# Batch 0's value projection moved ahead of the first scores, and each unit's value transfer put first on SyncE's queue

## The reference

```python
s = attention(xn)             # 32 heads of 8, keys i-8 .. i+7 alone, scores weighted by distance
                              # softmax, times the values, then proj_w and proj_b
g = silu(moe(xn))             # each token's best of 8 experts (router_w), silu-gated, score
                              # sigmoid(max logit), plus a shared expert for all tokens
out = x + s * g
```

## Time and profile before

| what | us |
|---|---|
| median of 3 runs | 641.51 (639.12, 641.51, 642.87) |
| the profiled execution, own time | 641.16 |
| its span | 639.3 |
| PE busy in the span | 562.8 (88%) |
| DVE busy | 404.0 (63%) |
| ACT busy | 308.1 (48%) |
| POOL busy | 186.8 (29%) |

### The profile page before, as it was taken

One profiled execution on the slowest core, in us unless ns is written; L12 is line 12 of the kernel. 1 busy time (PEld: TensorE's weight loads), 2 busy tenths in 40 slices (PEclk: granted clock), 3 DMA queues, 4 the chain that ended last, 5 costly groups with the idle time before them and its releaser, 6 DMA issues. The chain is left out here.

```text
span 639.3 us, 10599 instructions
## 1 busy us (share of the span) xinstructions
PE 562.8 (88%) x3358; PEld 484.0 (76%) x3358; DVE 404.0 (63%) x853; ACT 308.1 (48%) x762; POOL 186.8 (29%) x160
## 2 busy tenths in 40 slices
PE   2879999969879999999999999999886868789865
PEld 1657888858757899898999898898775756677754
DVE  6655746886755455455455455456688888886773
ACT  1374654557773544543544634546454543635332
POOL 6000101147861011010010110014645545532230
PEclk9899999979998999999999999999989899989997
DMA  9415532112326667666567576443133333330110
GB/s 294 133 62 190 177 122 61 57 44 96 111 87 178 174 166 223 196 184 195 165 189 223 167 218 185 134 133 107 51 98 110 102 106 105 113 109 20 43 35 23
DMA packets 107370, 82.89 MB, mean 130 GB/s; under 512 B 42292, under 2 KB 104756, under 8 KB 107316
## 3 DMA queue, kind: packets, MB, share of 16 engines
q1 hardware_dynamic: 98628, 68.72, 36.6%
q0 software_dynamic: 3072, 8.39, 4.1%
q10 hardware_dynamic: 5616, 5.11, 2.3%
HBM read 59.12 MB, written 23.07 MB: 129 GB/s over the span
## 5 line engine op out<-in xcount | busy, mean ns | idle before, releaser
L425 POOL TENSOR_TENSOR Sx<-Sx,mx 128x752 f32<-128x752 f32 x64 | 93.7, 1464 | 414.9 <-DVE mx L725 414.8
L941 PE MATMUL psV<-VB,PTs 128*128 128x132 f32 x1024 | 137.3, 288 | 43.3 <-DMA VB<-v_dram 19.0
L941 PEld LDWEIGHTS psV<-VB,PTs 128*128 128x128 f32 x1024 | 130.1, 197 | 50.8 <-issue 50.0
L468 ACT ACTIVATE Or<-psV 32x128 f32<-32x128 f32 x256 | 68.5, 268 | 151.4 <-DVE rs L755 148.9
L916 PE MATMUL psS<-kBD,qBD 128*128 128x188 f32 x512 | 104.9, 329 | 0.0
L916 PEld LDWEIGHTS psS<-kBD,qBD 128*128 128x128 f32 x512 | 87.9, 195 | 10.8 <-issue 2.0
L747 DVE STREAM_TRANSPOSE PTs<-Sx 128x512 f32<-128x512 f32 x128 | 82.9, 685 | 1.0 <-ACT Sx L498 1.0
L991 PE MATMUL psM<-xT,EB 128*128 128x128 f32 x624 | 76.4, 276 | 0.0
L718 DVE TENSOR_TENSOR Sx<-psS,cst 128x752 f32<-128x752 f32 x64 | 59.7, 933 | 26.3 <-PE psS L916 26.2
L991 PEld LDWEIGHTS psM<-xT,EB 128*128 128x128 f32 x624 | 73.9, 192 | 2.1 <-ACT qBD L487 1.3
L732 DVE SCALAR_TENSOR_TENSOR ea<-et,psM 128x256 f32<-128x256 f32 x39 | 16.4, 421 | 76.3 <-PE psM L991 47.2
(11 more groups left out here) (107 smaller groups left out, 690.6 us busy)
## 6 DMA issues: line engine op xcount, KB each, us to landing
EB<-in_L_ffn_gate_w SPq DMA_DIRECT2D x39, 256.0 KB, 3.0
EB<-in_L_ffn_up_w SPq DMA_DIRECT2D x39, 256.0 KB, 3.5
EB<-in_L_ffn_down_w SPq DMA_DIRECT2D x39, 256.0 KB, 3.1
VB<-v_dram SPq DMA_DIRECT2D x256, 32.0 KB
stage<-xs_dram SPq DMA_DIRECT2D x39, 128.0 KB, 2.2
ys_dram<-yb ACTq DMA_DIRECT2D x39, 128.0 KB, 3.1
xs_dram<-blank SPq DMA_DIRECT2D x9, 512.0 KB, 3.1
v_dram<-vS SPq DMA_DIRECT2D x8, 512.0 KB, 3.0
```

Source lines behind the costliest of these rows:

```text
L425: nc.gpsimd.tensor_tensor(s, s, mx[n % 3][:, :].unsqueeze(2).broadcast_to([P, 2 * G, KW]), ALU.subtract).then_inc(a_sub, 1)
L468: return nc.scalar.activation(dst, src, ACT.Copy)
L941: last = mm(psV[:, j, at:at + HS * VW], PTs[n % 2][:, k, j, i, :], VB[n % 2][:, i, k, :, VW * j:VW * j + VW], start=k == 0, stop=k == 1)
```

## The change

It does two things. First, the 4 value tiles of batch 0 are projected ahead of step 0, behind q, k0 and k1, by PE and by ACT, and stand in the list of jobs at that place; steps 1 to 7 keep theirs. Second, from SP's step 10 on (n - 1 > 8), `spread_v(n-1)` is the first thing of SP's step and no longer the last. For n - 1 = 0 to 8 it stays where it was, behind `keep_v`.

```diff
--- before.py
+++ after.py
@@ -113,7 +113,7 @@
 def jobs_of(n):
 
     if n == -1:
-        return [("tp", 0), ("tp", 1), ("q", 0), ("k0", 0), ("k1", 0)]
+        return [("tp", 0), ("tp", 1), ("q", 0), ("k0", 0), ("k1", 0)] + [("v", t) for t in range(BT)]
     found = []
     h = n // UH + 1
     if h < NH and n % UH == 0:
@@ -130,7 +130,7 @@
     if n < U and n % UB < 6:
         found.append((("sg", "su", "sg", "su", "sd", "sd")[n % UB], n))
     found += [("xa", i) for i in pair_at(n, 0)[1:]]
-    if n < BATCH:
+    if 1 <= n < BATCH:
         found += [("v", t) for t in range(n * BT, n * BT + BT)]
     if n >= 4 and n % 2 == 0 and (n - 4) // 2 < T:
         found.append(("pr", (n - 4) // 2))
@@ -364,6 +364,8 @@
                 sp.dma_start(out_v[:, c * CT:(c + 1) * CT, :], XR[b].rearrange("p (t c) -> p t c", t=CT)).then_inc(d_st[b], 16)
 
             for n in range(LAST + 1):
+                if BATCH < n - 1 < U:
+                    spread_v(n - 1)
                 for c in result_at(n - 1):
                     store(c)
                     if c + 3 < NC:
@@ -387,7 +389,7 @@
                     load_weights(i)
                 if 0 <= n - 1 < BATCH:
                     keep_v(n - 1)
-                if 0 <= n - 1 < U:
+                if 0 <= n - 1 <= BATCH:
                     spread_v(n - 1)
                 if n == C_STEP:
                     for c in range(3):
@@ -561,6 +563,8 @@
             rows_of(1)
             for kind in ("q", "k0", "k1"):
                 qk_out(kind, 0)
+            for t in range(BT):
+                v_out(t)
             deviation(1)
 
             def score():
@@ -1006,6 +1010,8 @@
             pe.wait_ge(s_wq, 16)
             for kind in ("q", "k0", "k1"):
                 project(kind, 0)
+            for t in range(BT):
+                values(t)
             for n in range(LAST + 1):
                 if n < U:
                     scores(n)
```

## The result

The changed kernel takes 634.26 us (median of 4 runs, 633.25 to 634.84), the kernel before 640.91 us (4 runs, 639.12 to 642.87). The ratio is 0.9886, with a 95% interval of 0.9858 to 0.9915: faster by 1.1% by that ratio, and by 6.6 us (1.0%) between the two medians. The forecast was 635.0 us, in a range of 631.5 to 639.5.

What follows compares the result with a forecast made beforehand. DVE, with ACT's round trip, was taken to set the late steps, and PE the expert stage. Start 3.0 plus scatter stage 3.5 made 6.5 us, 641.5 - 6.5 = 635.0 us, range 631.5 to 639.5.

Steps and rivals of the forecast that it cites:

- Values at their new place: Before step 0: router-weight wait 0.5 us, four tiles at 0.95 us each, first scores end at 27.0, no delay.
- The other bound of a tile: Before step 0, at the lower clock: a tile takes 1.5 us, the first scores end 3.6 us late.
- slow end of the range for the start: Lower bound of the start's gain: 3.9 - 3.6 - 1.7 = -1.4 us.
- What leaves step 0: End of step 0: copies and stalled tiles leave, values of batch 1 start at 41.5, 3.9 us sooner; 3.0 after the clock.
- The clock's share: PE's thin step 1: half of the 1.7 us lost in a stretch at 0.50 clock, 0.9 us, off the start's gain.
- Transfers first, scatter stage: At 193.10: PE's product starts at 190.85 and keeps its clock, 3.9 us together; 3.5 taken, bounds 1.4 and 3.9.
- that takes 0.3 back: First expert tile: up_w lands at 197.7, 3.5 us after issue, where PE would want it at 197.4.
- Transfers first, late steps: 466 to 574 us: PE's 15.5 us of waits for VB go, DVE's 8.37 us steps stay, gain nothing.
- the late waits count: Rival: DVE's late steps hang on PE, so 15.5 us more go, 619.5 us; chance 0.05.
- the start gives nothing: Rival: half clock through the tiles, start gains about 0, 3.0 to 3.5 from the scatter stage, 638.2 us; chance 0.13.
- the scatter stall comes back: Rival: it returns as a wait for first expert weights or rows, 0 to 1.4 us gained there, 637.8 us; chance 0.10.
- The slower case: Rival: tiles at half clock delay the scores' chain, thin step 1 adds 1.7, nothing at 193 us, 646.8 us; chance 0.03.

Runs made afterwards that it cites:

- result in the gap: Changed kernel with DVE's silu and result moved between the inverse of the row sums and the division: 611.85 us, ratio 0.9537.
- silu alone in the gap: Changed kernel with only DVE's silu moved between the inverse of the row sums and the division, result left behind: 624.03 us in one run.
- values alone: Changed kernel with SP's loop as it was, so batch 0's values ahead of step 0 but transfers of values last: 638.54 us, ratio 0.9948.
- the kernel with the transfer 2.5 us later: Kernel before, transfers from unit 40 on also waiting for DVE's transposed output (a_OT), meant to issue VB about 2.5 us later: 688.78 us in one run.
- the delayed transfers: Kernel before, transfers also waiting for DVE's row-sum inverse (from unit 40): 649.94 us; transposed output (from unit 40): 688.78 us; division (units 42 to 54): 652.90 us.
- transfers-alone: Kernel before with only the edits in SP's loop, transfers of values first from step 10 on: 636.82 us, ratio 0.9937.
- step-17: Kernel before with the transfer of values first in step 17 alone, where SP waits for all scatters: 637.52 us in one run.
- step-41: Kernel before with transfers of values first from step 41 on alone: 640.74 us in one run.

## Why the prediction was right, point by point

**The size.** 6.5 us were forecast, and 6.6 are the difference of the medians. Against the profiles, on which the sum was built, the terms come to 7.9, so the forecast was 1.4 us short, and the medians hide it. That the medians agree to 0.1 us is luck: the kernel before alone had medians of 640.3 to 641.7 us in the sets of runs beside the experiments.

**Values at their new place.** Right. The router weights ended a wait of 0.58 us (0.5 forecast), the tiles took 0.95 us each, the first scores 1.6. PE finished them at 27.33, with an input that had come 0.9 us later than in the other profile. That the wait for the router weights was so short is luck too. With the same start it was 1.19, 2.14 and 2.67 us in three other kernels (result in the gap, silu alone in the gap, values alone), and in the last two the first scores began at 26.11 only, against 23.92 in the kernel before. From ACT's first copy of q to DVE's step 0 it was 8.3 to 9.9 us in the profiles with four tiles ahead, 7.9 to 9.0 with none and 7.4 with two, and leads counted from step 0 leave this out. So the router weights are a price of the four tiles, which the forecast had sized from a single profile.

The other bound of a tile was misread. Its 1.5 us came from the 3.05 us that 8 instructions of 272 columns took at 18.06, but the clock records of that profile begin at 20.18 only, and say full speed up to 23.6; the same 8 took 2.00 us in the values-alone kernel, whose records say full speed from 17.55 on. A tile wholly at the lower clock takes 1.8 us (37.89 to 39.73 in the kernel with the transfer 2.5 us later), so the slow end of the range for the start should have been lower than -1.4. Nothing in the forecast of 635.0 hangs on it.

**What leaves step 0.** Right in place and size: values of batch 1 from 41.59 (41.5 forecast), 3.1 us at step 2 (3.0). The clock's share was right for a doubtful reason. I had taken half of a stretch because 2.25 us of standing had left the clock alone. It did fall, and cost 1.0 us of the values' time and 0.7 of su's, the latter being hidden: on whether the clock would fall my reason was wrong, and the 1.0 us lies near my 0.9 only because part of the stretch fell on su. PE is busy for 2.7 of the 6 us from 34 to 40 in every kernel with four tiles ahead, and the clock fell in all four of their profiles, between 38.0 and 40.2 us. The rule that I had weighed (the Trainium skill, TensorE: Matmul & The Clock Gate, Part 1) says that the clock follows how busy the engine has been recently. The trace agrees with it on the fall; its price of 1.7 us for this step came to 1.0.

**Transfers first, scatter stage.** The mechanism was right to a hundredth, 190.85 less the lead. One term was mis-sized: "that takes 0.3 back", for the first expert weights. They were issued at 191.05 and PE took them at 194.22 without a wait, so they had landed within 3.2 us, and the median of 3.5 us over all 39 such transfers was too long for this place. 3.9 us and not 3.5. A further 0.4 us came between steps 10 and 18, for which I had no term. It is no gain of the change: with the values alone it is 0.4 too, and with the transfers first from step 41 on, where nothing differs from the kernel before up to there, still 0.3. The one profile of before was slow there, as were those of four other kernels, which win 0.1 us or less in these steps.

**Transfers first, late steps.** Forecast nothing, measured nothing from 20 to 56, and 0.8 us at steps 57 to 58, which I had not seen. At 567.69 PE's last wait for VB, 2.50 us, ended just ahead of two steps in which PE has q, k and two shared-expert pieces and stands only 0.57 us more; DVE then waited 1.01 us for PE there. Timelines of PE and then DVE, kernel before; after the change DVE's operation at the second place follows on without a wait (577.39):

```profile
567.69 2.08 PE L941 MATMUL psV<-VB,PTs 128*128 128x132 f32 x16 [2.50 <-DMA VB<-v_dram]
...
585.34 0.69 DVE L784 SCALAR_TENSOR_TENSOR hTs<-ag,psM 128x512 f32<-128x512 f32 x1 [1.01 <-PE psM L968]
```

The step of the prediction that failed is "the 15.5 us of PE's waits for VB go, and DVE's 8.37 us steps stay: nothing": the last of those waits cost 0.8 us in the two steps behind the stretch that I had looked at. I had called the slack 2.1 us from one light step; the delayed transfers show that heavy steps have less.

**The rivals.** That the late waits count is out by the transfers-alone, step-17 and step-41 kernels. That the start gives nothing, and that the scatter stall comes back, are out by the two parts run alone. The slower case did not arise: no half clock in the tiles.

## What to carry to other kernels

A wait's sum says who stood, not what it costs. Ask when the next engine in line came to need the result: only the wait that held that engine too (here 1 of 6, and a part of the last) pays when it goes. Before filling a gap, ask what the moved work itself waits for: here it was the router weights, for 0.6 to 2.7 us. Before moving a transfer, look for the engine whose starts keep an even beat, and for what that engine itself waits: here DVE's own work, moved into a gap of 1.2 us and out from under POOL's combine, was worth three times the whole change. And queue order counts most where one queue holds an unrelated long wait, such as that for all scatters.

## What the runs showed of the hardware

DVE's multiplication in the result (X<-xnT,X, two SBUF tiles of 128x512, f32) takes 0.65 to 0.69 us alone. Where POOL's addition of the same size (1.28 us by itself) ran beside it, it took 1.4 to 2.5 us, and its end came 0.55 to 0.56 us behind the end of POOL's operation in all 73 such pairs of the 14 traces, whether POOL had begun up to 0.78 us before it or up to 0.62 us after it. So its length is what POOL's end leaves it, and what it had run before POOL began counts for nothing: 0.62 + 1.28 + 0.56 = 2.46 us in the step shown above. The Trainium skill, SBUF — State Buffer, section SBUF: two separate sides, says that DVE operations with two SBUF inputs and GpSimd operations that read SBUF lock a shared pair of ports, that the one that starts first has it for its whole instruction, and that the other blocks fully. The traces agree that one blocks fully, but not on which: this multiplication lost also where the profile has it start first. DVE's silu operation (xnT<-EB,xnT, also two SBUF tiles) kept its 0.65 us in 12 of 14 such meetings, and there it was POOL's operation that took longer, 1.38 to 1.68 us. What decides between the two the traces don't show. An operation of DVE with one SBUF and one PSUM input (ag<-tg,psM) took its 0.69 us where POOL's addition began inside it.

The lower TensorE clock is not a fixed tax on a place in the program. Once its first occasion was filled, it moved 14 to 17 us on (from 23.6 us to between 38.0 and 40.2), and with two tiles left in step 0 it did not come in the first 128 us, in either kernel of that kind. Nor does one start always meet it in the same way: of the eight profiles of kernels whose start is that of the kernel before, two had a second stretch at the lower level, from 38.0 us, and their step 1 came 1.7 us later for it. The times of four and of two tiles can't be told apart.
